# Inverse square roots as one power on GpSimd, in a four-stream stack of gated attention and FFN blocks

## What is computed

```python
def _layernorm(x, axis=-1, eps=1e-05):
    m = jnp.mean(x, axis=axis, keepdims=True)
    v = jnp.var(x, axis=axis, keepdims=True)
    return (x - m) / jnp.sqrt(v + eps)

x = x + jnp.tanh(g_xattn[l]) * xattn_l(_layernorm(x), ctx, ctx)
x = x + jnp.tanh(g_ffn[l]) * ffn_l(_layernorm(x))
```

```python
def rmsnorm(x):
    var = jnp.mean(jnp.square(x), axis=-1, keepdims=True)
    return x * jax.lax.rsqrt(var + 1e-06)
def activation_quant(x):
    scale = 127.0 / jnp.clip(jnp.max(jnp.abs(x), axis=-1, keepdims=True), EPS, None)
    return jnp.clip(jnp.round(x * scale), -128, 127) / scale
```

## Time and profile before

| | before |
|---|---|
| median of three runs | 2626.75 us (2623.39 to 2628.63) |
| span of the profiled execution | 2625.2 us |
| PE busy | 2472.9 us, 94% |
| DVE busy | 1491.8 us, 57% |
| ACT busy | 1204.5 us, 46% |
| POOL busy | 1170.3 us, 45% |
| mean granted TensorE clock | 0.992 |

### The profile page before, as it was taken

One profiled execution on the slowest core, in us unless ns is written; L12 is line 12 of the kernel. 1 busy time (PEld: TensorE's weight loads), 2 busy tenths in 40 slices (PEclk: granted clock), 3 DMA queues, 4 the chain that ended last, 5 costly groups with the idle time before them and its releaser, 6 DMA issues.

```text
span 2625.2 us, 53630 instructions
## 1 busy us (share of the span) xinstructions
PE 2472.9 (94%) x21300; PEld 1670.9 (64%) x21300; DVE 1491.8 (57%) x3948; ACT 1204.5 (46%) x1930; POOL 1170.3 (45%) x2521
## 2 busy tenths in 40 slices
PE   8999888999999988899999998899999999889998
PEld 5676445777776644577777655467767765447776
DVE  7555787545433687754543467874543257876442
ACT  5535477322244547723224546762322545674221
POOL 2334644545343554444533355444534345545442
PEclk9999999999999999999999999999999999999999
DMA  3200100000000000000000000000000000000000
GB/s 130 84 12 12 76 14 2 1 9 9 9 9 12 12 1 14 2 6 12 1 9 20 1 12 1 12 1 9 9 9 9 12 1 12 1 1 1 5 5 9
DMA packets 16279, 37.37 MB, mean 14 GB/s; under 512 B 1408, under 2 KB 11424, under 8 KB 15008
## 3 DMA queue, kind: packets, MB, share of 16 engines
q1 hardware_dynamic: 16032, 33.94, 3.7%
HBM read 29.74 MB, written 4.19 MB: 13 GB/s over the span
## 4 chain that ended last, share of the span: by engine, by line
PE 74%; DVE 14%; ACT 5%; POOL 4%; issue 3%; DMA 0%; DVEq 0%; POOLq 0%; ACTq 0%
PE P L1431 8%; PE P L1239 4%; PE P L1247 4%; PE P L1140 4%; PE P L1464 4%; PE P L1440 4%; PE P L1449 4%; PE P L1313 4%; PE P L1432 4%; PE P L1300 4%; PE P L1288 4%; PE P L1219 4%; DVE mx L1849 4%; ACT ET L1585 2%; PE P L1109 2%
## 5 line engine op out<-in xcount | busy, mean ns | idle before, releaser
L1849 DVE TENSOR_REDUCE mx<-P 128x8 f32<-128x1232 f32 x256 | 367.7, 1436 | 195.8 <-PE P L1136 63.5
L872 POOL TENSOR_SCALAR sm<-sm 128x1 f32<-128x1 f32 x512 | 174.6, 353 | 457.9 <-DVE sm L1845 457.4
L1431 PE MATMUL P<-xT,w 128*128 128x256 f32 x1024 | 265.6, 382 | 1.5 <-DVE sm L2042 0.8
L1543 ACT ACTIVATE xn<-x,sm 128x256 f32<-128x256 f32 x256 | 139.5, 593 | 228.3 <-POOL sm L878 228.2
L1885 DVE SCALAR_TENSOR_TENSOR x<-P,w_first,x 128x512 f32<-128x512 f32 x96 | 71.9, 749 | 290.7 <-PE P L1465 109.1
L1431 PEld LDWEIGHTS P<-xT,w 128*128 128x128 f32 x1024 | 190.3, 190 | 51.7 <-issue 25.9
L1585 ACT ACTIVATE ET<-P 128x2048 f32<-128x2048 f32 x96 | 180.1, 1876 | 68.1 <-PE P L1222 46.4
L1663 ACT ACTIVATE gu<-P 128x256 f32<-128x256 f32 x128 | 49.0, 383 | 331.1 <-PE P L1432 311.0
L1140 PE MATMUL P<-KB,R 32*128 32x308 f32 x1536 | 156.5, 476 | 39.0 <-ACT ET L1585 16.2
L2072 DVE SCALAR_TENSOR_TENSOR gu<-gu,P 128x256 f32<-128x256 f32 x128 | 53.7, 419 | 215.9 <-ACT gu L1663 215.6
L1219 PE MATMUL P<-R,KB 32*128 32x256 f32 x2048 | 162.3, 403 | 8.3 <-DVE mx L1849 8.3
(11 more groups left out here) (310 smaller groups left out, 5583.7 us busy)
## 6 DMA issues: line engine op xcount, KB each, us to landing
kvw<-in_wkv SPq DMA_DIRECT2D x12, 672.0 KB, 4.0
x<-in_x SPq DMA_DIRECT2D x16, 256.0 KB, 2.9
out<-x SPq DMA_DIRECT2D x16, 256.0 KB, 2.1
w<-in_w SPq DMA_DIRECT2D x2, 1024.0 KB, 6.3
w<-in_wexp SPq DMA_DIRECT2D x1, 1028.0 KB, 7.8
w_w<-in_wcon SPq DMA_DIRECT2D x1, 1024.0 KB, 10.1
w_w<-in_m3t SPq DMA_DIRECT2D x1, 1024.0 KB, 8.6
w<-in_w1q SPq DMA_DIRECT2D x1, 1024.0 KB, 10.6
```

The source lines that it names most:

```text
L872: own(e.tensor_scalar(a[:, i:i + 1], y[:, i:i + 1], y[:, i:i + 1], hv[:, i:i + 1], ALU.mult, ALU.mult), 1)
L1431: e.matmul(o, wm[:, c, js], s.xT[:, c, :], start=n == c == 0, stop=False, skip_group_check=True)
L1849: e.tensor_reduce(s.mx[:, i, :, 2 * u:2 * u + 2], quad[:, :, 0:2 * NK].rearrange("p g (a k) -> p g a k", a=2), AX.X, ALU.max).then_inc(q_d, 1)
```

## The change

The bit guess and the iterations are replaced by one instruction of POOL, a tensor_tensor with the operation power, whose exponents are -0.5 from a constant tile `root`. POOL also takes over the epsilon; nb becomes two products straight from the mean. DVE's norm ends with bn_aggr. In the quantised FFN the sums of squares become a step `sq` of their own on ACT and POOL, and DVE's `gelu2` becomes two steps, `am` (the maximum) and `fin` (the scales), between which other steps can stand. `am` and `sq` may run side by side. The durations in `parts` are changed with it (in ns: DVE norm from 1750 to 1150, gelu2 from 5700 to am 2300 and fin 1100; ACT gelu2 from 4400 to gelu2 1500 and sq 2900; POOL norm from 2600 to 1700, sq 1300), and all strings of `TURN` are new (not shown), SP's among them. Constants of waits on `g_const` rise by one for the new memset.

```diff
+        root = sb("root", [128, 2])
...
-        R_S = (0.375 / 0.703952253 ** 2) ** (1 / 7)
-        R_BITS, R_V, R_1 = 1595932665.0, -0.703952253 * R_S, 0.703952253 * 2.38924456 * R_S
-        R_2, R_3 = 1.25 / (R_S ** 4 * 0.703952253), 1.875 / R_S
...
                         yield "gelu2", s
+                        yield "name", "g"
+                        yield "am", s
+                        yield "name", "m"
+                        yield "need", "g"
+                        yield "sq", s
+                        yield "name", "y"
+                        yield "need", "m", "y"
+                        yield "fin", s
                         yield "rd", s, 0
...
+            e.memset(root[:], -0.5).then_inc(g_const, 1)
...
             def norm(s, b, k):
...
+                ve, a, y, nb = (s.sm[:, n, 0:2] for n in (0, 1, 2, 6))
+                v = s.mv[:, :, 1]
                 e.wait_ge(s.d_r, C.up(s.d_r))
-                for n in range(2):
-                    for i in range(2):
-                        own(e.tensor_scalar(a[:, i:i + 1], y[:, i:i + 1], y[:, i:i + 1], hv[:, i:i + 1], ALU.mult, ALU.mult), 1)
-                    if n:
-                        for i in range(2):
-                            own(e.tensor_scalar(a[:, i:i + 1], a[:, i:i + 1], R_2, a[:, i:i + 1], ALU.add, ALU.mult), 1)
-                    for i in range(2):
-                        own(e.tensor_scalar(y[:, i:i + 1], a[:, i:i + 1], (R_1, R_3)[n], y[:, i:i + 1], ALU.add, ALU.mult), 1 - i * n)
-                e.tensor_tensor(nb, m, y, ALU.mult).then_inc(s.g_r, 1)
+                if k < 6:
+                    own(e.tensor_scalar(ve, v, 1e-5, 1.0, ALU.add, ALU.mult))
+                else:
+                    own(e.tensor_scalar(a, v, 1e-5, 1e-6, ALU.add, ALU.mult))
+                    own(e.tensor_tensor(ve, v, a, ALU.add))
+                own(e.tensor_tensor(y, ve, root[:], ALU.pow))
+                for i in range(2):
+                    t = e.tensor_scalar(nb[:, i:i + 1], s.mv[:, i, 0:1], y[:, i:i + 1], -1.0, ALU.mult, ALU.mult)
+                t.then_inc(s.g_r, 1)
+
+            def sq(s):
+                hv, y, ss = (s.sm[:, n, 0:2] for n in (0, 3, 10))
+                e.wait_ge(s.a_d, C.up(s.a_d, 21) - 17)
+                own(e.tensor_scalar(hv, ss, 1.0 / 1024.0, 1e-6, ALU.mult, ALU.add))
+                e.tensor_tensor(y, hv, root[:], ALU.pow).then_inc(s.g_r, 1)
...
             def gelu2(s):
                 e.wait_ge(s.d_w, C.up(s.d_w, 4))
                 e.activation(s.h, s.h, ACT.Gelu).then_inc(s.a_d, 1)
-                e.wait_ge(s.a_d, C.up(s.a_d))
+                C.up(s.a_d)
+
+            def sq(s):
+                C.up(s.g_r)
+                e.wait_ge(s.a_d, C.at(s.a_d))
                 for i in range(2):
                     e.activation(s.qt, s.h[:, i, :], ACT.Square, accum_out=s.sm[:, 10, i:i + 1]).then_inc(s.a_d, 1)
                     e.wait_ge(s.a_d, C.up(s.a_d))
...
                 for i in range(2):
-                    e.wait_ge(d_own, C.at(d_own) - 1)
-                    e.bn_aggr(s.mv[:, i, :], s.st6[:, i, :]).then_inc(d_own, 1)
-                    C.up(d_own)
-                e.wait_ge(d_own, C.at(d_own))
...
-                e.tensor_scalar(y.bitcast(i32), a.bitcast(i32), -1.0, R_BITS, ALU.mult, ALU.add).then_inc(s.d_r, 1)
+                    e.wait_ge(d_own, C.at(d_own) - 1 + i)
+                    t = e.bn_aggr(s.mv[:, i, :], s.st6[:, i, :])
+                t.then_inc(s.d_r, 1)
...
+            def am(s):
                 e.wait_ge(s.a_d, C.up(s.a_d))
+                C.up(s.a_d, 2)
+                e.tensor_reduce(s.sm[:, 11, 0:2], s.h, AX.X, ALU.max, apply_absolute_value=True).then_inc(d_own, 1)
                 C.up(d_own)
...
+            def fin(s):
+                y, f, sq, am2 = (s.sm[:, n, 0:2] for n in (3, 8, 9, 11))
+                e.wait_ge(d_own, C.at(d_own))
+                e.wait_ge(s.g_r, C.up(s.g_r))
                 for i in range(2):
+                    e.tensor_scalar(am2[:, i:i + 1], am2[:, i:i + 1], y[:, i:i + 1], 1e-5, ALU.mult, ALU.max).then_inc(d_own, 1)
+                e.wait_ge(d_own, C.up(d_own, 2))
+                e.reciprocal(f, am2).then_inc(d_own, 1)
+                e.tensor_scalar(sq, am2, wsc[:, 7:8], None, ALU.mult)
+                e.wait_ge(d_own, C.up(d_own))
```

More of the change, by code:

```diff
@@ L267, in parts @@
             dve = {"grow": (160, 190, 230, 350, 620, 620, 620)[of[-1]] if name == "grow" else 0, "gb": 2500, "near": 420, "wide": 3200, "upt": 700, "tsum": 2300, "tern": 4700, "masks": 2800,
-                   "val": 850, "norm": 1750, "mx": 1390, "no": 1800 if l == 0 else 750, "nz": 950, "out": 770,
-                   "down": 770, "gate1": 620, "top1": 2700, "lin": 880, "q1": 2500, "w1": 670, "gelu2": 5700,
+                   "val": 850, "norm": 1150, "mx": 1390, "no": 1800 if l == 0 else 750, "nz": 950, "out": 770,
+                   "down": 770, "gate1": 620, "top1": 2700, "lin": 880, "q1": 2500, "w1": 670, "am": 2300, "fin": 1100,
                    "q2": 1420, "w2": 420, "gate3": 1350, "top3": 1600, "exa": 1700, "h1": 800, "h2": 800, "e3": 1200,
@@ L273, in parts @@
                    "turn": 600, "qp": 600 if l == 0 else 760, "mt": 350, "st": 500, "sts": 1100, "ex": 1800, "pv": 560,
-                   "up": 860, "gate1": 200, "gate3": 200, "tl": 400, "q1": 500, "gelu2": 4400, "q2": 1000, "rd": 2400, "mw": 600,
+                   "up": 860, "gate1": 200, "gate3": 200, "tl": 400, "q1": 500, "gelu2": 1500, "sq": 2900, "q2": 1000, "rd": 2400, "mw": 600,
                    "h1": 360, "h2": 360, "norm": 1000, "no": 900}
-            pool = {"split": 1500, "key": 1500, "mw": 1650, "norm": 2600, "bias": 1550, "hw": 2050,
+            pool = {"split": 1500, "key": 1500, "mw": 1650, "norm": 1700, "sq": 1300, "bias": 1550, "hw": 2050,
                     "no": 1250, "nz": 2350}
@@ L576, in build @@
[L576 to L580, removed]
@@ L627, in build @@
+            "SP": "0303000102300001023000010230000123",
         }
@@ L825, in pool_program @@
             e.wait_ge(l_first, 16 * len(FIRST))
-            e.wait_ge(g_const, 7)
+            e.wait_ge(g_const, 8)
             def sums(pb, of):
@@ L835, in sums, with own @@
                                     ALU.mult).then_inc(of, 1)
+            def own(t):
+                t.then_inc(g_own, 1)
+                e.wait_ge(g_own, C.up(g_own))
             sums(1, g_const)
@@ L898, in split @@
                 e.wait_ge(s.g_z, C.at(s.g_z))
-                def own(t):
-                    t.then_inc(g_own, 1)
-                    e.wait_ge(g_own, C.up(g_own))
                 if l == 3:
@@ L956, in hw @@
                 C.up(s.g_p)
-            stages = {"key": key, "norm": norm, "split": split, "bias": bias, "no": no, "nz": nz, "mw": mw, "hw": hw}
+            stages = {"key": key, "norm": norm, "sq": sq, "split": split, "bias": bias, "no": no, "nz": nz, "mw": mw, "hw": hw}
             for name, *of in ORDER["POOL"]:
@@ L1817, in norm @@
             def norm(s, b, k):
-                ve, a, y, m = (s.sm[:, n, 0:2] for n in (0, 1, 2, 5))
                 C.up(s.a_xn, 2)
+                C.up(s.g_r)
                 if k == 0:
@@ L1992, in w1_ @@
                                        op1=ALU.add).then_inc(s.d_w, 1)
-            def gelu2(s):
-                hv, a, y, f, sq, ss, am2 = (s.sm[:, n, 0:2] for n in (0, 1, 3, 8, 9, 10, 11))
-                def own(t, of):
-                    t.then_inc(d_own, 1)
-                    e.wait_ge(d_own, C.up(d_own) - of)
+            def am(s):
                 e.wait_ge(s.a_d, C.up(s.a_d))
-                e.tensor_reduce(am2, s.h, AX.X, ALU.max, apply_absolute_value=True).then_inc(d_own, 1)
+                C.up(s.a_d, 2)
+                e.tensor_reduce(s.sm[:, 11, 0:2], s.h, AX.X, ALU.max, apply_absolute_value=True).then_inc(d_own, 1)
@@ L2006, in gelu2 @@
                 C.up(d_own)
-                e.wait_ge(s.a_d, C.up(s.a_d, 2))
-                own(e.tensor_scalar(hv, ss, 1.0 / 1024.0, 1e-6, ALU.mult, ALU.add), 0)
-                own(e.tensor_scalar(a.bitcast(i32), hv.bitcast(i32), 1, None, ALU.logical_shift_right), 0)
-                own(e.tensor_scalar(hv, hv, R_V, None, ALU.mult), 1)
-                own(e.tensor_scalar(y.bitcast(i32), a.bitcast(i32), -1.0, R_BITS, ALU.mult, ALU.add), 0)
-                for n in range(2):
-                    for i in range(2):
-                        own(e.tensor_scalar(a[:, i:i + 1], y[:, i:i + 1], y[:, i:i + 1], hv[:, i:i + 1], ALU.mult, ALU.mult), 1)
-                    if n:
-                        for i in range(2):
-                            own(e.tensor_scalar(a[:, i:i + 1], a[:, i:i + 1], R_2, a[:, i:i + 1], ALU.add, ALU.mult), 1)
-                    for i in range(2):
-                        own(e.tensor_scalar(y[:, i:i + 1], a[:, i:i + 1], (R_1, R_3)[n], y[:, i:i + 1], ALU.add, ALU.mult), 1)
@@ L2021, in gelu2 @@
-                for i in range(2):
```

(12 more changed lines are left out.)

127 lines of the change are left out of this document (57 added, 70 removed).

## The result

The changed kernel took 2562.89 us (median of four runs, 2562.38 to 2564.5) against 2625.97 in the same call: ratio 0.9759, 95% interval 0.9746 to 0.9773, 63 us faster. The forecast was 2600 with a range of 2568 to 2632: right in sign, wrong in size, and outside the range.

What follows compares the result with a forecast made beforehand. Latency in four windows was taken to bound the kernel, PE being busy elsewhere; half of the chain's 63.2 us and the streams' 41.5 us, mean 26, took 2625.2 to 2599, stated as 2600, range 2568 to 2632.

Steps and rivals of the forecast that it cites:

- What bounds the kernel: Four windows with streams in layers 1 and 2 lose 120.8 us idle, 175.9 with fills, to latency; dense stretches gain nothing.
- I expect nothing from [the clock]: Granted clock already 0.98 to 1.00 of the 2.4 GHz level in every window shown; no gain expected.
- PE's useful busy sum stays: Expected sign on PE: useful busy time unchanged while the four windows shorten by 5 to 8 us each.
- One norm, step by step: In each norm, POOL takes 1.77 us for 3.29 and DVE loses 0.59: xn on ACT can begin 2.11 us earlier.
- The quantised layer: Second scaling of the quantised layer: 1.35 us in place of 2.23 on DVE, 0.88 less latency; 7.4 us of chain.
- The new orders I cost at nothing: New instruction orders of all engines: worth nothing beyond the shorter steps, as every engine issues what it did.
- first rival: Everything passes: all 63.2 us of the chain's shorter steps show in the span, giving 2563.5 us; chance 0.12.
- I let half pass in both: Half of the chain sum (31.6 us) and of the stream sum (20.8 us) reaches the span, mean 26 us.
- The power is slow: POOL's power in norms and scalings exceeds 0.8 us, each us beyond costing 31.2; 2660 at 5 us; chance 0.11.
- The break-even at 2.8 us: Length of POOL's power from which, at 31.2 us per us, the chain's 63.2 us gain would be gone.
- The port: DVE tensor_scalar meeting a POOL power waits to its end: 115 us possible blocking, 16 us seen by the chain.
- second rival: Other waits take over and DVE is blocked at the port shared with POOL: 2616 us; chance 0.18.

Runs made afterwards that it cites:

- run 1: The kernel before, in its old orders and planner durations, with all of the new POOL and DVE arithmetic; 2588.18 us, ratio 0.9849.
- run 14: The kernel before, in its old orders, with all of the new arithmetic and one unused power more in each norm; 2586.36 us, ratio 0.9845.
- run 10: The kernel before, in its own orders, with one unused power on POOL ahead of the iterations in each norm; 2679.38 us, ratio 1.0194.
- runs 4 and 6: The kernel after with one and with two unused powers ahead of the real one in each norm; 2583.25 and 2638.60 us.

## Why the prediction was wrong

The forecast was 26 us of gain; 63 were measured. Two terms of the sum make up the difference: the part of the shorter steps that passes (26 put, 40 measured in run 1) and the new orders (0 put, 25 measured). (40 and 25 don't add up to 63 exactly because runs of different calls are compared.)

- **What bounds the kernel**: right in the main. About 43 of 57 us less of idle and fill lie in the four windows, some 11 in each where 5 to 8 were put. The dense stretches, where nothing was expected, gave 6. PE's longest wait is now for the maximum of the scores, 16.6 us, as was said.
- **"I expect nothing from [the clock]"** and "PE's useful busy sum stays": not quite. It is some 8 us smaller, and the granted clock over the span 0.994 for 0.992. How much of the 8 us is the clock no run tells apart.
- **One norm, step by step**: right. 1.59 us on POOL for 1.77, the power 0.722 for 0.8.
- **The quantised layer**: too small. 7.4 us of chain, half of it passing; 12 to 14 measured in the new orders, where the step is also split, and 5.6, not clear of noise, in the old ones.
- **"The new orders I cost at nothing"**: the step that failed most. With the new arithmetic they bring 25 us (2588.2 to 2562.9; 24 by the ratios), and the intervals of the two ratios, 0.9832 to 0.9865 and 0.9746 to 0.9773, don't meet. I reasoned that every engine issues what it did and PE's total is the same. But an order is worth what its steps' durations make of it: the same new list with the old arithmetic is 76 us slower than before. The first rival's time came out, 2563, without its reason: its 63 us were to come from the shorter steps alone, and these gave 40. That the two figures agree is luck.
- **"I let half pass in both"**: the term was too small, and the form wrong. The arithmetic alone gave 40 us where 26 were put, 63% of the chain's 63.2; its time, 2588, is still within the forecast's own range of 2585 to 2612. But it doesn't pass in proportion: of 2.29 us a norm the last 0.8 give nothing in the old orders (run 14), and 0.8 more in the other direction cost 49 (run 10). The sum of a chain's pieces can't tell this.
- **"The power is slow"**: excluded, but its price per us, 31.2, was near only for the first 0.8 us in the new orders (25); beyond that it is 69, and in the old ones 0, 28 or 62. The break-even at 2.8 us was too generous for the new orders: by runs 4 and 6 the kernel is slower than before from somewhere between 0.8 and 1.6 us over the power's 0.72.
- **The port**: the loss of 16 us that the second rival put on DVE isn't seen: DVE's busy sum fell by more than the removed steps, 132 against 111. The trace of the kernel after also answers its mechanism. The instruction of line 1968 on DVE, once begun inside a power of POOL and once inside a bias addition:

```profile
343.56 0.70 POOL L884 TENSOR_TENSOR sm<-sm,root 128x2 f32<-128x2 f32 x1
343.59 0.18 DVE L1968 TENSOR_SCALAR sm<-sm 128x2 f32<-128x2 f32 x1
...
1028.30 1.27 POOL L895 TENSOR_TENSOR x<-x,w_bias 128x512 f32<-128x512 f32 x1
1028.47 1.38 DVE L1968 TENSOR_SCALAR sm<-sm 128x2 f32<-128x2 f32 x1
```

  The timeline has 46 single DVE instructions that begin inside a power, and none is more than 0.05 us longer than usual for its line; of 97 that begin inside an addition of line 895, 21 are longer by over 0.15 us. The port rule of the Trainium skill ("SBUF — State Buffer", Who interferes with whom), named beside that rival, has the first engine hold the shared pair for its whole instruction. By that, the trace agrees for the addition and not for the power of 0.70 us, beside which the DVE instruction took its usual 0.18.
- The sign, that the time lies in latency and not in an engine's total, was right for the stated reason.

What stays open: which of the moved steps make up the 19 us that the split doesn't explain. No run exchanges the order of one engine alone. No run has the old orders with the planner told the new durations either, so the share of the fills' places in the 25 us is only bounded by run 1's timeline.

## What to carry to other kernels

In a kernel whose engines run fixed interleaved lists, a step's latency has no single price: it is nearly free up to the slack that the order leaves and steep beyond, here 0, then 28 and then 62 us of kernel for each us of a norm in the old order. So a change that shortens a step has two parts, what the old order lets through (40 us) and what an order laid for the new durations adds (25 us), and the second is not to be costed at zero. A list laid for durations that turn out longer is worse than the old one: 76 us here.

## What was not expected of the hardware

A power of two elements in each of 128 partitions takes POOL 722 ns, 3.7 times its product of the same size (196 ns), and further ones in a row 693 to 710 (runs 4 and 6). DVE's small instructions that begin beside it keep their usual time, where beside a POOL addition of 512 elements one of 0.18 us takes 1.38. Taking 57 us of useless matmuls away made the kernel 17.5 us slower, at a granted clock of 0.985 in place of 0.994.
